# A selective-scan and expert block on one core: one more state scaled on ScalarE, one more product on GpSimd, the DMA queue and four copies re-ordered

## The chip, the core and the metric

The kernel runs on one core of one Trainium2 chip. The metric is the device time of one execution in microseconds (us); lower is better. The engines of the core run side by side and meet only at semaphores: TensorE (PE in the profile) multiplies matrices and transposes, VectorE (DVE) and ScalarE (ACT) work on tensors in the two on-chip memories SBUF and PSUM, GpSimd (POOL) on tensors in SBUF, and SyncE (SP) issues the DMAs. Each engine executes its own list of instructions in order, so an instruction that waits holds up everything behind it on its engine.

## The reference

The input x has 32 sequences of 512 tokens and 256 channels. It is normalised per token (xn), goes through a selective scan in both directions, and is gated by an expert feed-forward layer:

```python
dbc = einsum('bld,nd->bln', xn, x_proj_w); delta, B, C = split(dbc)      # 32 + 16 + 16
delta = softplus(einsum('blr,dr->bld', delta, dt_proj_w) + dt_proj_b)
h[t] = exp(delta[t] * A) * h[t-1] + delta[t] * B[t] * xn[t]              # 16 states, 256 channels
y    = sum over states (h * C) + D * xn       # forward, and again on the reversed sequence
out  = x + (y_forward + y_backward) * silu(ffn(xn))
```

`ffn` picks one of 8 experts per sequence (a router on the last token), and computes xn + 0.3 * ((gelu(xn W1 + b1) W2 + b2) Wo + bo). All of it is float32.

## The kernel before, in words

Channels lie on the 128 partitions in two halves (DT = 2), tokens along the free dimension, so one tensor for one state is 128x1024. There are 32 **sequences** (the code calls them rows), and in each of them 32 **states**, 16 forward and 16 backward, numbered 0 to 31. Each engine runs a loop over sequences and, inside, over 32 **steps** s; step s is mostly the work on state s. Into the steps the **front** of the next sequence is woven: its normalisation, its projections, its delta and its feed-forward layer. The tables at lines 37 to 49 say at which step each piece of the front is issued (a number of 32 or more is a step of the following sequence).

For one state the work is:

- **decay** (ACT, `make_decay`, L745): exp(delta * A), two instructions of 128x512, two states ahead of the scan. It goes to one of two PSUM buffers (`dps`, called decay in the profile), which is free once the scan two states earlier has ended; for a *turned* state it goes to SBUF (`decay_sb`).
- **bx** = delta * x * B, by one of two ways. For the states in POOL_B, GpSimd multiplies `dx` by a row of B that a DMA has spread over the partitions (`times_b`, L473). For the states in TURNED, ScalarE scales `dxT` (the transposed dx) by B in four instructions of 128x256 (`scale_dx`, L584, at the step that SCALED_AT gives) and TensorE transposes the result into the PSUM buffer (`turn_bx`, L1054, three steps ahead).
- **scan** (DVE, L849): h = decay * h + bx over the 1024 columns.
- **product with C**: for the states in ON_DVE, TensorE spreads C over the partitions of one PSUM bank (`broadcast_c`, L1062) and DVE multiplies (`times_c`, L827), after the scan of the next state. For the states in POOL_C, GpSimd multiplies with a row of C brought by a DMA (L461), four steps later in its own order.
- **sum** (PE, `add_state`, L1079): eight 128x128 matmuls add the product to y in PSUM.

The front pieces of one sequence share one PSUM bank, `fps` (front in the profile): TensorE fills it, ScalarE or VectorE copies it out, and only then does TensorE fill it again. The pieces that matter here, in their order: the expansion of delta for channel half q of the direction (`expand_delta`, L997 and L998), copied out by `absolute` (L592 writes |.| to ex, L596 writes the relu to delta); the feed-forward input (`ffn_in`, L1007), copied out by `hidden` (L619); and the transposes of dx (`turn_dx`, L983), copied out by `copy_dxT` (L574). On ScalarE, `drain` issues these copies at the start of a step, ahead of the decay and of `scale_dx`; `front` comes after them and holds the exp, ln and squares of softplus (L600, L605, L609, L613) and the gelu. On TensorE the front comes last in a step.

Ahead of the loops lies a prologue (from L698 on ScalarE): the router, the product W2 Wo for all eight experts (`turn_w2`, `times_wo`, `copy_w2o`), and the front of sequence 0.

SP issues all DMAs in one order: it walks over the states of POOL_B, loads B five products ahead and C three products ahead, each behind a wait for the product that frees the buffer, and at two places it adds the loads of the expert and the move of the projections (`move_bc`, which brings high and low into dbc).

## Time and profile before

| | |
|---|---|
| time, median of 3 | 3342.31 us (3339.49 to 3346.29) |
| the profiled execution | 3348.41 us, of which the trace spans 3346.6 us |
| DVE busy | 3116.1 us, 93% |
| POOL busy | 3010.0 us, 90% |
| ACT busy | 2908.7 us, 87% |
| PE busy (modelled ends) | 2561.6 us, 77% |
| mean granted TensorE clock | 0.916 of full speed |

DVE, POOL and ACT each have under 15% of the span in which they do nothing. Busy time that high on three engines means that the share alone does not tell what a change is worth: what tells it is which engine's wait ends last at the place that is changed. Mean times of one instruction are read from the rows below; on ACT, DVE and POOL an instruction starts some 0.1 us before the one ahead of it has ended, so the distance of two starts is the right cost of one.

### The profile page before, as it was taken

To read this page: it belongs to the slowest core of one execution; us is meant where nothing else is said; L and a number is where in the kernel's file an instruction comes from. 1 tells how busy PE (TensorE), PEld (TensorE's weight loads), DVE (VectorE), ACT (ScalarE), POOL (GpSimd) and SP (SyncE) were. 2 spreads that over 40 slices of the span, in tenths; PEclk is the share of its full clock that TensorE was granted. 3 is DMA by queue.
4 is the path that set the end of the run, shared out by engine and by line. 5 is a ranking of instruction groups with operands and counts; after the bars stand their busy time and mean duration, and the time that the engine had idled before them with its cause. 6 is when DMAs were issued, how large, how long until landed. Compare 5 with 4: busy or idle time off the path is not lost. (4 is left out here: it accounts for less than half of the span.)

```text
span 3346.6 us, 47865 instructions
## 1 busy us (share of the span) xinstructions
PE 2561.6 (77%) x15542; PEld 2049.9 (61%) x15542; DVE 3116.1 (93%) x2059; ACT 2908.7 (87%) x5370; POOL 3010.0 (90%) x1422
## 2 busy tenths in 40 slices
PE   7777777777777777777777777777777777777776
PEld 5666656666566665566666566666566665666665
DVE  2899999999999999999999999999999999999998
ACT  4888889989888888898888899898898888898985
POOL 2899999999998998999999999999999889999997
PEclk9898999899899988999889999988999889999888
DMA  5443344442344433434433444423434334344332
GB/s 155 137 125 104 100 138 121 128 124 88 119 131 125 125 109 95 132 121 128 125 103 101 136 122 125 126 91 115 130 128 125 106 93 136 119 130 124 96 104 69
DMA packets 273358, 394.09 MB, mean 118 GB/s; under 512 B 45003, under 2 KB 119508, under 8 KB 273108
## 3 DMA queue, kind: packets, MB, share of 16 engines
q1 hardware_dynamic: 273108, 391.03, 38.1%
q8 instruction: 124, 2.03, 0.2%
q14 instruction: 126, 1.03, 0.1%
HBM read 348.98 MB, written 25.18 MB: 112 GB/s over the span
## 5 line engine op out<-in xcount | busy, mean ns | idle before, releaser
L473 POOL TENSOR_TENSOR bx<-dx,b_sb 128x1024 f32<-128x1024 f32 x640 | 1511.8, 2380 | 99.5 <-DVE hs L849 97.7
L849 DVE TENSOR_TENSOR_SCAN hs<-decay,bx 128x1024 f32<-128x1024 f32 x640 | 1458.0, 2280 | 25.5 <-ACT decay L745 8.5
L1079 PE MATMUL y<-ident,hc 128*128 128x128 f32 x8192 | 1145.4, 291 | 25.7 <-DVE hc L827 25.5
L1079 PEld LDWEIGHTS y<-ident,hc 128*128 128x128 f32 x8192 | 1029.9, 152 | 141.2 <-DVE hc L827 80.1
L461 POOL TENSOR_TENSOR hc<-hs,c_sb 128x1024 f32<-128x1024 f32 x416 | 981.0, 2369 | 13.2 <-DVE hs L849 12.9
L849 DVE TENSOR_TENSOR_SCAN hs<-decay_sb,decay 128x1024 f32<-128x1024 f32 x384 | 865.1, 2274 | 77.1 <-issue 38.0
L745 ACT ACTIVATE decay<-delta,rate 128x512 f32<-128x512 f32 (+1 forms) x1280 | 827.3, 683 | 62.1 <-DVE hs L849 61.7
L827 DVE TENSOR_TENSOR hc<-hs,c 128x1024 f32<-128x1024 f32 x608 | 728.7, 1199 | 40.7 <-PE c L1062 36.8
L584 ACT ACTIVATE dxb<-dxT,btok 128x256 f32<-128x256 f32 x1536 | 651.2, 497 | 0.5 <-PE decay L1054 0.5
L1054 PE MATMUL decay<-ident,dxb 128*128 128x128 f32 x3072 | 435.5, 288 | 252.8 <-DVE hs L849 246.4
L1054 PEld LDWEIGHTS decay<-ident,dxb 128*128 128x128 f32 x3072 | 359.7, 147 | 367.5 <-issue 272.7
L1062 PE MATMUL c<-dbc,selector 128*128 128x512 f32 x608 | 327.0, 538 | 324.8 <-DVE hc L827 324.7
L745 ACT ACTIVATE decay_sb<-delta,rate 128x512 f32<-128x512 f32 (+1 forms) x768 | 506.2, 715 | 0.0
L1062 PEld LDWEIGHTS c<-dbc,selector 128*128 128x128 f32 x608 | 125.1, 206 | 407.8 <-DVE hc L827 389.7
L1023 PE MATMUL front<-w2o_sb,hT 128*128 128x256 f32 x1024 | 287.0, 430 | 77.9 <-issue 77.9
L1023 PEld LDWEIGHTS front<-w2o_sb,hT 128*128 128x128 f32 x1024 | 214.7, 221 | 114.2 <-issue 84.4
L1007 PE MATMUL front<-xnT,w_sb 128*128 128x512 f32 x512 | 249.9, 611 | 44.0 <-ACT delta L596 42.8
L448 POOL TENSOR_TENSOR lg<-lg,ex 128x1024 f32<-128x1024 f32 x64 | 151.1, 2362 | 86.9 <-ACT lg L613 86.9
L592 ACT ACTIVATE ex<-front,dtb 128x512 f32<-128x512 f32 x128 | 87.3, 682 | 100.0 <-PE front L998 99.6
L574 ACT ACTIVATE dxT<-front 128x512 f32<-128x512 f32 x128 | 75.8, 592 | 103.3 <-PE front L983 103.1
L619 ACT ACTIVATE hT<-front,b_sb 128x512 f32<-128x512 f32 x128 | 87.7, 685 | 87.3 <-PE front L1007 87.3
L1007 PEld LDWEIGHTS front<-xnT,w_sb 128*128 128x128 f32 x512 | 88.3, 192 | 121.6 <-issue 63.1
(127 smaller groups left out, 2294.4 us busy)
## 6 DMA issues: line engine op xcount, KB each, us to landing
b_sb<-b_scratch SPq DMA_DIRECT2D x640, 256.0 KB, 3.4
c_sb<-b_scratch SPq DMA_DIRECT2D x416, 256.0 KB, 3.6
xin<-in_L_attn_x_dram SPq DMA_DIRECT2D x32, 512.0 KB, 7.7
w_sb<-in_L_ffn_W_dram SPq DMA_DIRECT2D x32, 512.0 KB, 4.3
w2o_sb<-w2o_scratch SPq DMA_DIRECT2D x32, 512.0 KB
xres<-in_L_attn_x_dram SPq DMA_DIRECT2D x32, 512.0 KB, 5.4
out_dram<-og SPq DMA_DIRECT2D x32, 512.0 KB, 4.4
dbc<-high SPq DMA_DIRECT2D x64, 128.0 KB, 5.6
```

The costliest lines, as they stand in the source:

```text
L448: nc.gpsimd.tensor_tensor(lg[:, :, :], lg[:, :, :], ex[:, g, :, :], ALU.mult).then_inc(s_log1p, 1)
L461: nc.gpsimd.tensor_tensor(hc[:, s % RING, :, :], hs[:, s % HSLOTS, :, :], c_sb[:, i % CRING, :].unsqueeze(1).broadcast_to([P, DT, T]), ALU ...
L473: nc.gpsimd.tensor_tensor(bx[:, i % RING, :, :], dx[:, g, :, :], b_sb[:, i % BRING, :].unsqueeze(1).broadcast_to([P, DT, T]), ALU.mult).th ...
L584: A(dxb[:, (row * NT + i) % XSLOTS, c, :], dxT[:, g, c, :], ACT.Copy, scale=btok[:, par, c, g, n:n + 1]).then_inc(s_dxb, 1)
L745: A(to[:, k, cols], delta[:, g * (1 + par), k, cols], ACT.Exp, scale=rate[:, g, k, n:n + 1]).then_inc(s_decay, 1)
L827: V.tensor_tensor(hc[:, s % RING, :, :], hs[:, s % HSLOTS, :, :], cps[:, :].unsqueeze(1).broadcast_to([P, DT, T]), ALU.mult).then_inc(s_hc, 1)
L849: V.tensor_tensor_scan(hs[:, s % HSLOTS, :, :].rearrange("p k t -> p (k t)")[:, u], factor.rearrange("p k t -> p (k t)")[:, u], data.rearr ...
L1007: ins = M(fps[:, :], w1_sb[:, k, j * P:(j + 1) * P], xnT[:, par, k, :], start=(k == 0), stop=(k == DT - 1))
L1023: M(to, hT[:, j, c * P:(c + 1) * P], w2o_sb[:, j, :], start=(j == 0), stop=False)
L1054: ins = nc.tensor.transpose(dps[s % DSLOTS][:, k, c * P:(c + 1) * P], dxb[:, (row * NT + i) % XSLOTS, c, k * P:(k + 1) * P], ident[:, :])
L1062: M(cps[:, :], selector[:, N + n:N + n + 1].broadcast_to([P, P]), dbc[:, par, g, :], start=True, stop=True).then_inc(s_cps, 1)
L1079: ins = M(yps[:, c, k * P:(k + 1) * P], hc[:, s % RING, k, c * P:(c + 1) * P], ident[:, :], start=False, stop=(s == ADDED[-1]), is_transpo ...
```

## The change

State 20 joins TURNED (12 states become 13, scaled at step 15), so its bx moves from GpSimd to ScalarE and TensorE. State 17 joins POOL_C (13 become 14), so its product with C moves from DVE to GpSimd. Four copies out of the shared bank move: the two of the forward delta (ABS 16 and 17) from the start of their step to behind the decay and the scaling, HIDDEN's last from step 24 to 25, and the first two of DX_COPY from 30 and 31 to 31 and 32. SP's loop now walks over all 32 steps in GpSimd's order, and `move_bc` comes at step 14. In the prologue the gelu of sequence 0 goes behind the first two decays, the router's exp ahead of the first softplus, and the loads of the dt weights ahead of those of W2 and Wo. Lines behind the edits shift by 1 to 3.

```diff
-    DX_TURN, DX_COPY = (28, 29, 44, 45), (30, 31, 46, 47)
-    FFN_IN, HIDDEN, GELU = (16, 16, 18, 18, 20, 20, 22, 22), (18, 20, 22, 24), 31
+    DX_TURN, DX_COPY = (28, 29, 44, 45), (31, 32, 46, 47)
+    FFN_IN, HIDDEN, GELU = (16, 16, 18, 18, 20, 20, 22, 22), (18, 20, 22, 25), 31
...
-    TURNED, SCALED_AT, TURN_LEAD = (..., 15, 22, 24, 28, 30), (..., 10, 17, 19, 23, 25), 3
+    TURNED, SCALED_AT, TURN_LEAD = (..., 15, 20, 22, 24, 28, 30), (..., 10, 15, 17, 19, 23, 25), 3
-    POOL_C, C_LAG, ADD_LAG = (2, 4, 5, 7, 9, 10, 11, 12, 16, 18, 20, 26, 27), 4, 2
+    POOL_C, C_LAG, ADD_LAG = (2, 4, 5, 7, 9, 10, 11, 12, 16, 17, 18, 20, 26, 27), 4, 2
...
-            sp.dma_start(w2_in[0][:, :, :], w2_v[0]).then_inc(s_w2[0], 16)
-            sp.dma_start(wo_sb[:, :, :], wo.rearrange("(k p) n -> p k n", p=P)).then_inc(s_wo, 16)
             sp.wait_ge(s_dtz, 1)
...
+            sp.dma_start(w2_in[0][:, :, :], w2_v[0]).then_inc(s_w2[0], 16)
+            sp.dma_start(wo_sb[:, :, :], wo.rearrange("(k p) n -> p k n", p=P)).then_inc(s_wo, 16)
...
-                for i in range(NBX):
-                    j = i + BRING - 1
...
-                    for s in POOL_C:
-                        ahead = POOL_C.index(s) + C_AHEAD
-                        if on_bx(s) == i and ahead < NPC:
-                            load_c(row, par, ahead)
+                for s in range(STEPS):
+                    if s in POOL_B:
+                        j = on_bx(s) + BRING - 1
...
+                    if s - C_LAG in POOL_C:
+                        i = on_pool(s - C_LAG) + C_AHEAD
+                        if i < NPC:
+                            load_c(row, par, i)
...
-                    if POOL_B[i] == 16 and not last:
+                    if s == 14 and not last:
...
             def drain(row, par, s):
-                if s in DX_COPY:
+                if s in DX_COPY and (row or s in DX_COPY[DT:]):
                     copy_dxT(row, DX_COPY.index(s))
-                if s in ABS:
+                if s in ABS[DT:]:
                     absolute(row, par, ABS.index(s))
...
             def front(row, par, s):
...
+                if s in ABS[:DT]:
+                    absolute(row, par, ABS.index(s))
                 if s in EXP:
...
             absolute(0, 0, 1)
+            act.wait_ge(s_rv, 6)
+            A(lexp[:, :], router_ps[0:NB, 384:384 + NE], ACT.Exp, bias=lneg[:, :], accum_out=lsum[:, :]).then_inc(s_ra, 1)
             exp_abs(0, 0)
...
-            gelu(0)
-            act.preload_act_table_set(exp_ln)
             def make_decay(row, par, s):
...
             make_decay(0, 0, 1)
+            gelu(0)
+            act.preload_act_table_set(exp_ln)
```

How this changes the order on two engines, at steps 16 to 20 of a sequence. On ScalarE before, from the first copy of the forward delta (ex and delta are its two halves) to the decay of state 20 (decay0 and decay1 are the two PSUM buffers, dxb the scaled dx of state 22, hT the first piece of the feed-forward input):

```order
L592 ACTIVATE ex<-front,dtb 128x512
L596 ACTIVATE delta<-front,dtb 128x512
L745 ACTIVATE decay0<-delta,rate 128x511
L745 ACTIVATE decay0<-delta,rate 128x512
L592 ACTIVATE ex<-front,dtb 128x512
L596 ACTIVATE delta<-front,dtb 128x512
L745 ACTIVATE decay1<-delta,rate 128x511
L745 ACTIVATE decay1<-delta,rate 128x512
L584 ACTIVATE dxb<-dxT,btok 128x256 x4
L619 ACTIVATE hT<-front,b1_sb 128x512
L745 ACTIVATE decay0<-delta,rate 128x511
L745 ACTIVATE decay0<-delta,rate 128x512
```

The two pairs L592 and L596 stand ahead of the decays of states 18 and 19; between the second pair and hT there are a decay and a scaling. Now, on the same engine, from the decay of state 18 on:

```order
L746 ACTIVATE decay0<-delta,rate 128x511
L746 ACTIVATE decay0<-delta,rate 128x512
L593 ACTIVATE ex<-front,dtb 128x512
L597 ACTIVATE delta<-front,dtb 128x512
L746 ACTIVATE decay1<-delta,rate 128x511
L746 ACTIVATE decay1<-delta,rate 128x512
L585 ACTIVATE dxb<-dxT,btok 128x256 x4
L593 ACTIVATE ex<-front,dtb 128x512
L597 ACTIVATE delta<-front,dtb 128x512
L620 ACTIVATE hT<-front,b1_sb 128x512
L743 ACTIVATE decay_sb<-eps 128x1
L746 ACTIVATE decay_sb<-delta,rate 128x511
```

The second pair now stands directly ahead of hT, behind the decay of state 19 and the scaling of state 22, and the decay of state 20 goes to SBUF and has a small edge instruction (L743) of its own. On VectorE before, from the scan of state 16 to that of state 20 (the five L849 rows), with the products of states 15 and 17 between them:

```order
L849 SCALAR_TENSOR_TENSOR hs<-decay0,bx 128x1024
L827 TENSOR_TENSOR hc<-hs,c 128x1024
L849 SCALAR_TENSOR_TENSOR hs<-decay1,bx 128x1024
L849 SCALAR_TENSOR_TENSOR hs<-decay0,bx 128x1024
L827 TENSOR_TENSOR hc<-hs,c 128x1024
L849 SCALAR_TENSOR_TENSOR hs<-decay1,bx 128x1024
L849 SCALAR_TENSOR_TENSOR hs<-decay0,bx 128x1024
```

The fifth row is the product of state 17. Now the same engine from state 16 on:

```order
L852 SCALAR_TENSOR_TENSOR hs<-decay0,bx 128x1024
L830 TENSOR_TENSOR hc<-hs,c 128x1024
L852 SCALAR_TENSOR_TENSOR hs<-decay1,bx 128x1024
L852 SCALAR_TENSOR_TENSOR hs<-decay0,bx 128x1024
L852 SCALAR_TENSOR_TENSOR hs<-decay1,bx 128x1024
L852 SCALAR_TENSOR_TENSOR hs<-decay_sb,decay0 128x1024
```

The product is gone, and the scans of states 17 to 20 stand in a row; that of state 20 takes its decay from SBUF and its bx from the PSUM buffer.

## Rows read from the trace of the kernel before

**Rows 1.** The page's part 1: busy time, share of the span, instructions.
```profile
PE 2561.6 (77%) x15542; PEld 2049.9 (61%) x15542; DVE 3116.1 (93%) x2059; ACT 2908.7 (87%) x5370; POOL 3010.0 (90%) x1422
```

**Rows 2.** Waits by engine and releaser: us in total, times, longest us.
```profile
ACT hT L619 <- PE front L1007: 87.3, 37, 3.8
...
DVE hc L827 <- PE c L1062: 36.8, 33, 1.9
...
DVE zz L802 <- PE front L1025: 19.1, 33, 3.3
```

**Rows 3.** The page's part 5: busy us, mean ns; idle before, releaser.
```profile
L473 POOL TENSOR_TENSOR bx<-dx,b_sb 128x1024 f32<-128x1024 f32 x640 | 1511.8, 2380 | 99.5 <-DVE hs L849 97.7
L849 DVE TENSOR_TENSOR_SCAN hs<-decay,bx 128x1024 f32<-128x1024 f32 x640 | 1458.0, 2280 | 25.5 <-ACT decay L745 8.5
...
L849 DVE TENSOR_TENSOR_SCAN hs<-decay_sb,decay 128x1024 f32<-128x1024 f32 x384 | 865.1, 2274 | 77.1 <-issue 38.0
```

**Rows 4.** Durations at their extremes, by line: ns min/median/max, first and last start.
```profile
L820 DVE TENSOR_TENSOR og<-y,gate x32: 1198/1198/1226, 198.2 to 3339.5; 128x1024 f32<-128x1024 f32 x32
...
L849 DVE TENSOR_TENSOR_SCAN hs<-decay,bx x640: 2258/2282/2292, 84.3 to 3333.1; 128x1024 f32<-128x1024 f32 x160
```

**Rows 5.** Order of time, VectorE, 448 to 464 us: start, us, instruction, idle.
```profile
448.30 4.46 DVE L849 TENSOR_TENSOR_SCAN hs<-decay,bx 128x1024 f32<-128x1024 f32 x2
452.68 1.20 DVE L827 TENSOR_TENSOR hc<-hs,c 128x1024 f32<-128x1024 f32 x1
453.80 4.67 DVE L849 TENSOR_TENSOR_SCAN hs<-decay,bx 128x1024 f32<-128x1024 f32 x2
...
463.02 2.29 DVE L849 TENSOR_TENSOR_SCAN hs<-decay_sb,decay 128x1024 f32<-128x1024 f32 x1 [1.25 <-ACT decay_sb L745]
```

**Rows 6.** Order of time, ScalarE, the same stretch.
```profile
447.88 0.69 ACT L592 ACTIVATE ex<-front,dtb 128x512 f32<-128x512 f32 x1 [2.38 <-PE front L998]
...
450.26 0.68 ACT L592 ACTIVATE ex<-front,dtb 128x512 f32<-128x512 f32 x1
450.83 0.69 ACT L596 ACTIVATE delta<-front,dtb 128x512 f32<-128x512 f32 x1
451.40 1.31 ACT L745 ACTIVATE decay<-delta,rate 128x511 f32<-128x511 f32 x2
452.62 1.70 ACT L584 ACTIVATE dxb<-dxT,btok 128x256 f32<-128x256 f32 x4
454.22 0.68 ACT L619 ACTIVATE hT<-front,b_sb 128x512 f32<-128x512 f32 x1
...
461.39 0.21 ACT L742 ACTIVATE decay_sb<-eps 128x1 f32<-128x1 f32 x1
461.49 1.34 ACT L745 ACTIVATE decay_sb<-delta,rate 128x511 f32<-128x511 f32 x2
```

**Rows 7.** Order of time, TensorE, the same stretch.
```profile
451.57 1.98 PE L1007 MATMUL front<-xnT,w_sb 128*128 128x512 f32 x4 [1.34 <-ACT delta L596]
```

**Rows 8.** Order of time, all engines, the prologue.
```profile
10.76 0.66 PE L1106 MATMUL c<-ident,decay_sb 128*128 128x128 f32 x2 [10.76 <-DMA decay_sb<-_L_attn_dt_proj_b_w_dram]
...
45.48 0.15 DVE L900 RECIPROCAL lrec<-lsum 32x1 f32<-32x1 f32 x1 [5.68 <-ACT lexp L704]
...
78.08 1.29 DVE L858 COPY hc<-y 128x512 f32<-128x512 f32 x2 [7.68 <-PE y L1089]
...
84.30 2.29 DVE L849 TENSOR_TENSOR_SCAN hs<-decay,bx 128x1024 f32<-128x1024 f32 x1 [4.93 <-ACT decay L745]
```

**Rows 9.** The same matmuls at the half clock, and core 0's mean clock.
```profile
1060.58 3.45 PE L1007 MATMUL front<-xnT,w_sb 128*128 128x512 f32 x4 [1.41 <-ACT delta L596]
...
core 0: 3346.6 us, clock 0.916
```

**Rows 10.** Order of time, all engines, around a sequence's last state.
```profile
1102.21 0.60 ACT L574 ACTIVATE dxT<-front 128x512 f32<-128x512 f32 x1 [3.09 <-PE front L983]
...
1104.92 1.22 DVE L827 TENSOR_TENSOR hc<-hs,c 128x1024 f32<-128x1024 f32 x1 [1.11 <-PE c L1062]
```

More of the change, by code:

```diff
@@ L396, in body @@
                 first, second_last = isinstance(row, int) and row == 0, isinstance(row, int) and row == NB - 2
-                for i in range(NBX):
-                    j = i + BRING - 1
-                    if j < NBX:
-                        load_b(row, par, j)
-                    elif not last:
-                        load_b(row + 1, 1 - par, j - NBX)
-                    for s in POOL_C:
-                        ahead = POOL_C.index(s) + C_AHEAD
-                        if on_bx(s) == i and ahead < NPC:
-                            load_c(row, par, ahead)
-                        elif on_bx(s) == i and not last:
-                            load_c(row + 1, 1 - par, ahead - NPC)
-                    if POOL_B[i] == 10:
+                for s in range(STEPS):
+                    if s in POOL_B:
+                        j = on_bx(s) + BRING - 1
+                        if j < NBX:
+                            load_b(row, par, j)
+                        elif not last:
+                            load_b(row + 1, 1 - par, j - NBX)
+                    if s - C_LAG in POOL_C:
+                        i = on_pool(s - C_LAG) + C_AHEAD
+                        if i < NPC:
+                            load_c(row, par, i)
+                        elif not last:
+                            load_c(row + 1, 1 - par, i - NPC)
+                    if s == 10:
                         if not first:
@@ L425, in _ @@
         def _(pool):
+            nc.gpsimd.memset(dtw_raw[:, :, :, :], 0.0).then_inc(s_dtz, 1)
             nc.gpsimd.memset(ident[:, :], 0.0).then_inc(s_ident0, 1)
```

5 lines of the change are left out of this document (1 added, 4 removed).

## The prediction

> **What bounds the kernel now.** I read the busy shares first [rows 1]: VectorE 93%, GpSimd 90%, ScalarE 87%. The reader is to see that VectorE leads and that no engine has much room. Next came the waits [rows 2]: ScalarE waits 87.3 us for TensorE's feed-forward input, VectorE 36.8 us for the C that TensorE spreads and 19.1 us for the gate input. The costliest groups [rows 3] add that GpSimd's products with B wait 97.7 us for VectorE's scans, and that VectorE's scans have 25.5 and 77.1 us of idle ahead of them. So VectorE leads and the others mostly follow it. The 32 gate products `og` start between 198.2 and 3339.5 us [rows 4], so a sequence costs (3339.5 - 198.2) / 31 = 101.3 us.
>
> Then I read one sequence in order of time, where the change is, at 448 to 464 us [rows 5 to 7], on three engines. On VectorE, 448.30 x2 are the scans of states 17 and 18; 452.68 is the product of state 17, the one that the change takes away; 453.80 x2 are the scans of 19 and 20; behind those follow the product of 19 and state 21, and at 463.02 state 22, after 1.25 us of idle put down to ScalarE's decay. So at this place ScalarE's list, not VectorE, sets when state 22 starts. On ScalarE [rows 6] no instruction after 447.88 shows idle time ahead of it: pair L592/L596, decay 18, pair, decay 19, scaling of 22, hT, decay 20 and so on up to the decay of 22 at 461.49. The place is a local bound by ScalarE inside a kernel that VectorE bounds elsewhere.
>
> **The change part by part.** Distances of starts are the costs [rows 5, 6]: a product on VectorE 453.80 - 452.68 = 1.12 us; on ScalarE a pair of copies 451.40 - 450.26 = 1.14, a decay 452.62 - 451.40 = 1.22, a scaling 454.22 - 452.62 = 1.60, an edge instruction 461.49 - 461.39 = 0.10.
>
> *State 17's product leaves VectorE, state 20's bx leaves GpSimd, state 17's product joins GpSimd.* GpSimd is even. VectorE has 1.12 us less per sequence, all of it between the scans of 18 and 19. ScalarE gets four scalings, 1.60 us, at step 15, ahead of the decay of 18; that lies in the 2.38 us in which it waited for the first pair [rows 6], so it costs nothing by itself.
>
> *The copies of the forward delta move behind the decays.* This is the term that decides. I go through the same sequence with the new order. The decay of 18 now comes before the first pair, in the old idle time. The decay of 19 goes to the PSUM buffer that the scan of 17 reads, so it starts when that scan ends: 448.30 + 2.28 = 450.58. Then the scaling of 22 at 451.80, the second pair at 453.40, its relu half at 453.97 (0.57 later, as from 450.26 to 450.83). Before, that half started at 450.83. TensorE's first feed-forward group waits for this half: it started 451.57 - 450.83 = 0.74 after it and took 1.98 us [rows 7]. Before, that lay beside the decay of 19 and the scaling of 22. Now nothing stands between the pair and hT: hT is the next instruction of the list and waits for those matmuls, to 453.97 + 0.74 + 1.98 + 0.04 = 456.73. It stood at 454.22 [rows 6]: 2.51 us late. Behind it, in order, are the decay of 20, exp, the decay of 21, the scaling of 24, ln, the second hT and the decay of 22, which is what state 22 waits for. The decay of 20 also gets an edge instruction, 0.10. State 22 then starts at 463.02 + 2.51 + 0.10 = 465.63, 2.6 us later. On VectorE the three scans 18, 19 and 20 stand in a row: with 2.2 us each from 450.5 (448.30 + 4.46 - 2.26) the scan of 19 is over at 454.9. State 20's started at 453.80 + 4.67 - 2.28 = 456.19 and now starts at 456.19 + 2.61 = 458.8, so VectorE waits 3.9 us there, and the 1.12 us that the product gave up are inside this wait. 31 sequences have such a stretch (the last one has no next front): 31 x 2.61 = +81.
>
> *What that wait swallows.* Scans fed from bx have 25.5 us of idle ahead of them [rows 3], of which 4.93 belong to the first scan [rows 8]. The other 20.6 are waits of states 18, 20 and 26, which come from late pieces of the same chain; the new order puts the decay of 18 first and HIDDEN's last copy behind the decay of 26. I take all of it off: -21. The bounds are 0 and 21.
>
> *The half clock.* The mean granted clock is 0.916 [rows 9], so (1 - 0.916) x 2 = 17% of the time is at 1.2 GHz. There the group of matmuls that is now exposed takes 3.45 us and not 1.98 [rows 7, 9]: 31 x 0.17 x 1.47 = +8, between 0 and twice that.
>
> *The last sequence* saves its product: -1.
>
> *The two DX_COPY.* The first stood at step 30 and waited 3.09 us for its transposes [rows 10]; at step 31 it comes behind a decay (1.3 with its edge) and a square (1.1) and lands at about the same time. Zero, because ScalarE's idle time hides it; if that cover were gone, the product of state 31, which has 1.11 us of idle ahead of it [rows 10], would come later by what the copy is late, at most some 0.5 us per sequence, +16. The reordering of HIDDEN's last copy is in the 21 above.
>
> *SP's order.* It issues the same DMAs. `move_bc` now waits for less, but what it feeds, the first pair, is no longer what is late. What holds GpSimd's products with B up is a scan in 97.7 of 99.5 us [rows 3], not a DMA, and the new order asks for each buffer when GpSimd has freed it. Zero; queued behind a wait in it are the B and C rows of the steps ahead, five and three products early.
>
> *The prologue.* The first scan waits 4.93 us for its decay behind the gelu and its two table loads, and VectorE is free after the copy that ends at 79.37 [rows 8]. It will start up to 4.6 us earlier; but the gelu now lies ahead of the decay of state 2, and gives most of it back. The router's exp comes four softplus instructions earlier, where VectorE waited 5.68 us, and TensorE's first transposes waited to 10.76 us for the dt weights, which now load ahead of W2. Bounds: 0, and 4.93 + 5.68 + half of 10.76 = -16. I take -6, nearer to the lower end since each of the three meets the next wait.
>
> **Sum**: 81 - 21 + 8 - 1 - 6 = +61 us. Against the profiled execution, 3348.4 us (span 3346.6 and 1.8 around it), that is 3409. The median of the runs is 6.1 below the profiled one, so the median should be 3342.3 + 61 = 3403 us, 1.8% slower.
>
> **The rivals.**
>
> *VectorE's relief counts in full* (the other side). The one mechanism: hT does not wait, because the wait at state 20 stays below what VectorE has gained. The place is the stretch of rows 5, the price is 32 x 1.12 = -36 us plus -6 in the prologue, and it decides from the point where hT starts less than 1.1 us later than it did, that is, if the pair would stand at 452.0 and not at 453.4. For it: the busy shares, where VectorE leads. Against it: ScalarE's list stands in a fixed order, and its costs are all from rows. 3342 - 42 = 3300 us.
>
> *The late start is made up later*. The stretch is late by 2.6 us, but VectorE waits elsewhere as well: 36.8 us for the spread C and 19.1 for the gate input [rows 2]. If these fell to nothing and the prologue gave its full 16 us: 61 - 56 - 10 = -5, about 3337 to 3345. Against it: most of them come from chains that start at a scan of VectorE and so move with it.
>
> *The moved product stops VectorE.* Both engines read SBUF, and a GpSimd product of 2.37 us more beside the scans could hold a scan up for its length. In the trace 640 scans take 2258 to 2292 ns [rows 4] beside a GpSimd that is busy 90% of the time [rows 1], so no such hold is seen. If each of the 32 moved products did hold one up: 32 x (2.37 - 1.12) = +40, about 3382 us with the stretch as it was. The Trainium skill (Perfetto Trace Analysis, section "Optimizing Scalar/DVE Operations") warns that VectorE and GpSimd share a read port, so that moving work between those two might not help; by that rule the move of the product is worth nothing or less, and the trace does not bear it out for these operand kinds.
>
> *The change does not do what it says*: the order of the two kernels shows that it does, so this has no chance of its own.
>
> **How the numbers follow.** The forecast, a new wait ahead of state 20, has 77%. Its own range goes from +26 (the waits for C fall to their floor of about 0.65 us, the 0.48 us matmul and its hand-over, and those for the gate input vanish: 61 - 17 - 19) to +90 (no cover, half clock twice as frequent): 3365 to 3432 us, which I take to hold nine in ten of it. VectorE's relief in full 13%, made up later 5%, the moved product or a starved queue 5%. The range is to leave out no more than two in ten: 3330 to 3430. About 0.2% (7 us) is what a measurement of this kernel can tell from no change. Faster comes from the relief, 13%; the same from the case that is made up, 5%; slower from the rest, 82%.
>
> **What the profile after would show.** Right: idle time ahead of the scans that read decay_sb grows from 77.1 us [rows 3] by about 31 x 3.9 = 120 us, put down to ScalarE's decay_sb or to issue; in a sequence the scan of 20 starts some 8.2 us after the end of the scan of 17, and that of 22 some 15.0 after it, against 5.6 and 12.4; ScalarE waits about 2 us for TensorE ahead of the first hT of each sequence, and no longer ahead of the first pair; VectorE's busy time falls by 36 us. GpSimd's idle time grows by 2 us a sequence. Right for the other steps: the first scan starts near 79 us or before. Wrong: if no wait over 1 us stands ahead of state 20's scan, the term of 81 is wrong; if it stands there and the sequence is still not longer than 101.3 us, what swallows it is what I left out.

## The result and the profile after

The changed kernel takes 3455.81 us (median of 4 runs, 3451.8 to 3457.05) against 3344.3 us of the kernel before (4 runs, 3339.49 to 3356.89): 1.0325 times as long, 95% interval 1.0295 to 1.0356. That is 111 us more, where 61 were forecast. The sign was right; the time lies 26 us above the range's upper end. The times and ratios in this document leave out a second, longer time that one kernel showed: two of the five runs of e1_copies_ahead, the traced one among them, took 3365 us and not 3312, for a reason that no run here tells.

The page's part 1 of the changed kernel, as in [rows 1], and its row of the granted clock in tenths, one digit for a fortieth of the span:

```profile
PE 2596.1 (75%) x15766; PEld 2061.1 (60%) x15766; DVE 3076.1 (89%) x2027; ACT 2983.1 (86%) x5498; POOL 3010.8 (87%) x1422
...
PEclk9989899899999899999989999988999899989998
```

VectorE lost 40 us of work (3116.1 to 3076.1) and its share fell from 93% to 89%: nothing on it got slower, it waits. Its waits come next, with those of the engines that it waits for: us in total, times, longest.

```profile
DVE hs L852 <- ACT decay_sb L746: 214.1, 64, 5.8
...
ACT hT L620 <- PE front L1010: 143.7, 64, 9.7
...
PE front L1010 <- ACT delta L597: 129.2, 31, 4.2
...
DVE hs L852 <- issue: 36.7, 63, 0.8
...
DVE hc L830 <- PE c L1065: 34.5, 28, 1.4
...
ACT ex L593 <- PE front L1001: 20.6, 34, 1.8
...
DVE zz L805 <- PE front L1028: 15.6, 27, 3.3
```

VectorE's waits for C and for the gate input are nearly what they were in [rows 2] (36.8 and 19.1). New is a chain of three: TensorE waits up to 4.2 us for the delta, ScalarE 143.7 us for TensorE's feed-forward input (87.3 before), and VectorE up to 5.8 us for ScalarE's decay. The costliest groups that answer to [rows 3], with busy us, mean ns, then idle time ahead of them:

```profile
L474 POOL TENSOR_TENSOR bx<-dx,b_sb 128x1024 f32<-128x1024 f32 x608 | 1435.7, 2377 | 89.3 <-DVE hs L852 89.1
L852 DVE TENSOR_TENSOR_SCAN hs<-decay,bx 128x1024 f32<-128x1024 f32 x608 | 1378.4, 2276 | 4.4 <-ACT decay L746 3.8
L462 POOL TENSOR_TENSOR hc<-hs,c_sb 128x1024 f32<-128x1024 f32 x448 | 1052.8, 2363 | 142.1 <-DVE hs L852 141.7
L852 DVE TENSOR_TENSOR_SCAN hs<-decay_sb,decay 128x1024 f32<-128x1024 f32 x416 | 937.6, 2273 | 250.5 <-ACT decay_sb L746 214.1
...
L1010 PE MATMUL front<-xnT,w_sb 128*128 128x512 f32 x512 | 300.2, 717 | 136.3 <-ACT delta L597 129.2
```

The idle time ahead of the scans that read decay_sb went from 77.1 to 250.5 us, ahead of those that read bx from 25.5 to 4.4. A scan takes what it took (2276 and 2273 ns against 2280 and 2274). State 20 counts among the readers of decay_sb only since the change; its waits are 178.8 of the 250.5 us. The last row is the group whose price the prediction had too low: TensorE's feed-forward matmuls take 717 ns each in the mean, and they took 611 before.

One sequence in order of time shows where that comes from. VectorE, as in [rows 5]: three scans in a row (states 17, 18, 19), 5.82 us of waiting ahead of state 20, and 1.10 ahead of state 22.

```profile
458.17 6.64 DVE L852 TENSOR_TENSOR_SCAN hs<-decay,bx 128x1024 f32<-128x1024 f32 x3
470.63 2.29 DVE L852 TENSOR_TENSOR_SCAN hs<-decay_sb,decay 128x1024 f32<-128x1024 f32 x1 [5.82 <-ACT decay_sb L746]
...
477.33 2.29 DVE L852 TENSOR_TENSOR_SCAN hs<-decay_sb,decay 128x1024 f32<-128x1024 f32 x1 [1.10 <-ACT decay_sb L746]
```

ScalarE in the same stretch, as in [rows 6]. The second pair (463.32, 463.89) is directly followed by hT, which waits 3.87 us.

```profile
460.49 1.30 ACT L746 ACTIVATE decay<-delta,rate 128x511 f32<-128x511 f32 x2 [0.83 <-DVE hs L852]
461.73 1.69 ACT L585 ACTIVATE dxb<-dxT,btok 128x256 f32<-128x256 f32 x4
463.32 0.67 ACT L593 ACTIVATE ex<-front,dtb 128x512 f32<-128x512 f32 x1
463.89 0.67 ACT L597 ACTIVATE delta<-front,dtb 128x512 f32<-128x512 f32 x1
468.44 0.69 ACT L620 ACTIVATE hT<-front,b_sb 128x512 f32<-128x512 f32 x1 [3.87 <-PE front L1010]
469.02 0.19 ACT L743 ACTIVATE decay_sb<-eps 128x1 f32<-128x1 f32 x1
469.12 1.32 ACT L746 ACTIVATE decay_sb<-delta,rate 128x511 f32<-128x511 f32 x2
```

TensorE in it, as in [rows 7]. After its last small matmul at 460.06 it has nothing to do for 4.17 us, and then the four matmuls that all others wait for take 3.78 us, not 1.98.

```profile
460.06 0.39 PE L1001 MATMUL front<-dbc,dtw_low 128*128 128x512 f32 x1
464.62 3.78 PE L1010 MATMUL front<-xnT,w_sb 128*128 128x512 f32 x4 [4.17 <-ACT delta L597]
468.19 1.76 PE L1057 MATMUL decay<-ident,dxb 128*128 128x128 f32 x8
```

The same place by stretches: us, then busy time of TensorE, its weight loads, VectorE, ScalarE and GpSimd, the granted clock, DMA share, GB/s.

```profile
460.00:463.00 3.00, 0.45 (x2) 0.01 (x1) 3.00 (x3) 2.51 (x6) 3.00 (x2) 0.97 0.36 119
463.00:466.00 3.00, 1.38 (x2) 0.84 (x3) 1.81 (x1) 1.56 (x4) 3.00 (x2) 0.50 0.31 108
466.00:469.00 3.00, 3.00 (x7) 1.37 (x6) 0.00 (x0) 0.56 (x1) 2.82 (x2) 0.50 0.20 68
469.00:472.00 3.00, 3.00 (x18) 2.40 (x17) 1.36 (x1) 3.00 (x7) 0.00 (x0) 0.89 0.26 87
```

The granted clock is 0.97, then 0.50 (1.2 GHz) in two stretches of three microseconds each, and in them lie all four matmuls that the kernel waits for. In the kernel before it is 1.00 throughout this place, where TensorE idled 1.34 us:

```profile
448.00:451.00 3.00, 1.78 (x11) 1.31 (x11) 3.00 (x3) 3.00 (x6) 3.00 (x3) 1.00 0.44 139
451.00:454.00 3.00, 2.05 (x5) 0.75 (x6) 3.00 (x3) 3.00 (x7) 3.00 (x2) 1.00 0.04 16
```

The group is slow in every sequence. Of the 31 such groups of matmuls, 26 take 3.78 us in the changed kernel and the other five 3.26 to 3.51; in the kernel before, 27 took 1.98 or 1.99 and only four were slow (3.23 to 3.48). Yet the mean clock of the whole span hardly moved (0.916 before, 0.912 now). From the first scan of the second sequence to the first scan of the last one, thirty sequences on, a sequence now takes (3352.568 - 193.755) / 30 = 105.29 us, against (3242.964 - 191.656) / 30 = 101.71 before.

### The profile page after: what moved, and what is told of

The parts are those of the page before. It is cut to its first block and busy times, and to the rows that moved or that the text cites. A ratio compares the mean times of both kernels' runs of the same rounds, so it can differ in the third digit from the quotient of the medians.

```text
span 3455.1 us, 48409 instructions
## 1 busy us (share of the span) xinstructions
PE 2596.1 (75%) x15766; PEld 2061.1 (60%) x15766; DVE 3076.1 (89%) x2027; ACT 2983.1 (86%) x5498; POOL 3010.8 (87%) x1422
## 5 line engine op out<-in xcount | busy, mean ns | idle before, releaser
L474 POOL TENSOR_TENSOR bx<-dx,b_sb 128x1024 f32<-128x1024 f32 x608 | 1435.7, 2377 | 89.3 <-DVE hs L852 89.1
L852 DVE TENSOR_TENSOR_SCAN hs<-decay,bx 128x1024 f32<-128x1024 f32 x608 | 1378.4, 2276 | 4.4 <-ACT decay L746 3.8
L462 POOL TENSOR_TENSOR hc<-hs,c_sb 128x1024 f32<-128x1024 f32 x448 | 1052.8, 2363 | 142.1 <-DVE hs L852 141.7
L852 DVE TENSOR_TENSOR_SCAN hs<-decay_sb,decay 128x1024 f32<-128x1024 f32 x416 | 937.6, 2273 | 250.5 <-ACT decay_sb L746 214.1
L746 ACT ACTIVATE decay<-delta,rate 128x511 f32<-128x511 f32 (+1 forms) x1216 | 786.4, 680 | 180.8 <-DVE hs L852 180.4
L830 DVE TENSOR_TENSOR hc<-hs,c 128x1024 f32<-128x1024 f32 x576 | 689.5, 1197 | 39.8 <-PE c L1065 34.5
L585 ACT ACTIVATE dxb<-dxT,btok 128x256 f32<-128x256 f32 x1664 | 704.6, 495 | 0.0
L746 ACT ACTIVATE decay_sb<-delta,rate 128x512 f32<-128x512 f32 (+1 forms) x832 | 547.6, 712 | 0.0
L1010 PE MATMUL front<-xnT,w_sb 128*128 128x512 f32 x512 | 300.2, 717 | 136.3 <-ACT delta L597 129.2
L620 ACT ACTIVATE hT<-front,b_sb 128x512 f32<-128x512 f32 x128 | 87.0, 680 | 143.7 <-PE front L1010 143.7
L445 POOL TENSOR_TENSOR dx<-delta,xnT 128x1024 f32<-128x1024 f32 x64 | 151.9, 2373 | 2.5
L454 POOL TENSOR_TENSOR delta<-lg,delta 128x1024 f32<-128x1024 f32 x64 | 151.6, 2369 | 0.1
```

The source lines that it names most:

```text
L445: nc.gpsimd.tensor_tensor(dx[:, g, :, :], delta[:, g * (1 + par), :, :], xnT[:, par, :, :], ALU.mult).then_inc(s_dx, 1)
L462: nc.gpsimd.tensor_tensor(hc[:, s % RING, :, :], hs[:, s % HSLOTS, :, :], c_sb[:, i % CRING, :].unsqueeze(1).broadcast_to([P, DT, T]), ALU ...
L474: nc.gpsimd.tensor_tensor(bx[:, i % RING, :, :], dx[:, g, :, :], b_sb[:, i % BRING, :].unsqueeze(1).broadcast_to([P, DT, T]), ALU.mult).th ...
L585: A(dxb[:, (row * NT + i) % XSLOTS, c, :], dxT[:, g, c, :], ACT.Copy, scale=btok[:, par, c, g, n:n + 1]).then_inc(s_dxb, 1)
L746: A(to[:, k, cols], delta[:, g * (1 + par), k, cols], ACT.Exp, scale=rate[:, g, k, n:n + 1]).then_inc(s_decay, 1)
L830: V.tensor_tensor(hc[:, s % RING, :, :], hs[:, s % HSLOTS, :, :], cps[:, :].unsqueeze(1).broadcast_to([P, DT, T]), ALU.mult).then_inc(s_hc, 1)
```

## The experiments

Twelve kernels ran. They ask which part of the change costs the time, why it costs twice what was forecast, and what the parts are worth without it. Ratios are to the kernel before on the same chip, with 95% intervals.

### Which part costs the time

**e2_copies_only**: the kernel before with this part alone.

```diff
             def drain(row, par, s):
-                if s in ABS:
+                if s in ABS[DT:]:
                     absolute(row, par, ABS.index(s))
             def front(row, par, s):
+                if s in ABS[:DT]:
+                    absolute(row, par, ABS.index(s))
                 if s in EXP:
```

> The kernel before with one part added: the two copies of the forward delta behind the decay and the scaling; nothing else. Theory: this alone brings the whole loss, 31 x (16.8 - 12.9) = +120 us, 3440 to 3470 us, with the clock low while the first feed-forward matmuls run; if the clock were high there, 31 x 2.0 = +62, 3404 us. Rival (the states): within 20 us of the kernel before.

Measured: 3466.51 us, 1.0355 [1.0335, 1.0374]. This part alone brings the whole loss, as expected (3440 to 3470 us). The ratio is some 10 us above that of the full change, but the two intervals overlap. The trace has a trap for readers. Its wait is labelled with GpSimd's bx:

```profile
471.00 2.29 DVE L851 TENSOR_TENSOR_SCAN hs<-decay,bx 128x1024 f32<-128x1024 f32 x1 [4.46 <-POOL bx L473]
```

```profile
468.06 2.36 POOL L473 TENSOR_TENSOR bx<-dx,b_sb 128x1024 f32<-128x1024 f32 x1
```

```profile
469.04 0.69 ACT L619 ACTIVATE hT<-front,b_sb 128x512 f32<-128x512 f32 x1 [3.87 <-PE front L1009]
469.62 1.29 ACT L747 ACTIVATE decay<-delta,rate 128x511 f32<-128x511 f32 x2
```

The bx was ready at 468.06 + 2.36 = 470.42, the decay of state 20 at 469.62 + 1.29 = 470.91, and the scan starts at 471.00. So the scan follows ScalarE's decay, behind the same late hT, though GpSimd was only 0.5 us ahead of it.

**e1_copies_ahead**: the changed kernel with this part alone undone, so all the others remain.

```diff
-                if s in ABS[DT:]:
+                if s in ABS:
                     absolute(row, par, ABS.index(s))
...
-                if s in ABS[:DT]:
-                    absolute(row, par, ABS.index(s))
                 if s in EXP:
```

> The changed kernel with one part undone: the two copies of the forward delta stand at the start of steps 16 and 17 again, ahead of the decay and the scaling. Theory (the place of the copies): the first hT no longer waits for the matmuls, the wait ahead of state 20's scan falls from 5.8 us to under 1, state 22 starts 12.9 us after the end of the scan of 17 and not 16.9, and the kernel takes 3315 to 3340 us. Rival (the states that moved, through the four added scalings and state 20's decay in SBUF): the time stays above 3430 us.

Measured: 3312.57 us, 0.9897 [0.9878, 0.9917], 2 us below the range that was expected. Nothing is read from its trace. With e2 it brackets the part: -143 us if it is undone, +120 if it is done alone. The remaining parts together are worth some -34.

**e4_states_only**: the kernel before with the tables of states, 13 scaled on ScalarE and 14 products on GpSimd.

```diff
-    TURNED, SCALED_AT, TURN_LEAD = (..., 15, 22, 24, 28, 30), (..., 10, 17, 19, 23, 25), 3
+    TURNED, SCALED_AT, TURN_LEAD = (..., 15, 20, 22, 24, 28, 30), (..., 10, 15, 17, 19, 23, 25), 3
-    POOL_C, C_LAG, ADD_LAG = (..., 16, 18, 20, 26, 27), 4, 2
+    POOL_C, C_LAG, ADD_LAG = (..., 16, 17, 18, 20, 26, 27), 4, 2
```

> The kernel before with the tables of states alone changed: 13 states scaled on ScalarE, 14 products with C on GpSimd; all copies, the queue and the prologue as before. Theory (the stretch from the first copy to the decay of state 22 is bound by ScalarE's list): the 1.12 us less on VectorE per sequence brings nothing, since state 22 waits for ScalarE, and the scalings ahead of the first copy cost 0 to 0.4 us per sequence: 3340 to 3355 us. Rival (VectorE bounds the stretch): 31 x 1.1 = 35 us less, 3308 us.

Measured: 3349.23 us (10 runs), 1.0007 [0.9994, 1.0019]. VectorE's busy time falls to 3082.5 us, 34 less, and the time does not move. The answer is in one row: the idle time ahead of the scans that read decay_sb, state 20 now among them, went from 77.1 [rows 3] to 122.1 us. The edit moves the product and adds ScalarE's scalings at once, so it prices the two together and neither alone. It also isn't free of the clock: ten of the 31 feed-forward groups are slow in this trace (3.42 to 3.64 us), against four before. With such a group state 20 waits 2.1 to 2.4 us, without it 1.3, so six more of them are some 6 us.

```profile
L849 DVE TENSOR_TENSOR_SCAN hs<-decay_sb,decay 128x1024 f32<-128x1024 f32 x416 | 937.7, 2273 | 122.1 <-ACT decay_sb L745 79.1
```

**e5_queue_only**: the kernel before with SP's DMAs asked for in GpSimd's step order.

```diff
-                for i in range(NBX):
-                    j = i + BRING - 1
...
-                    for s in POOL_C:
-                        ahead = POOL_C.index(s) + C_AHEAD
-                        if on_bx(s) == i and ahead < NPC:
-                            load_c(row, par, ahead)
...
+                for s in range(STEPS):
+                    if s in POOL_B:
+                        j = on_bx(s) + BRING - 1
...
+                    if s - C_LAG in POOL_C:
+                        i = on_pool(s - C_LAG) + C_AHEAD
...
-                    if POOL_B[i] == 16 and not last:
+                    if s == 14 and not last:
```

> The kernel before with SP's loop in GpSimd's step order and the move of the projections at step 14. Theory (no DMA was late for GpSimd; only the projections come earlier, which in some sequences held the first copy of delta up by about 1 us): 0 to 15 us less, 3330 to 3345 us. Rival (a B or C row now comes late): 10 us or more slower.

Measured: 3328.3 us, 0.9958 [0.9945, 0.9971]: 14 us (0.42%) faster, where the prediction had zero and the expectation 0 to 15. Of the two edits, the loop and the earlier `move_bc`, no run tells which one gains. The idle time ahead of the scans that read bx fell from 25.5 to 13.6 us:

```profile
L850 DVE TENSOR_TENSOR_SCAN hs<-decay,bx 128x1024 f32<-128x1024 f32 x640 | 1455.2, 2278 | 13.6 <-ACT decay L746 8.9
```

**e6_prologue_only**: the kernel before with row 0's gelu behind the decay of state 1, the router's exp earlier, and the dt weights loaded ahead of W2 (with GpSimd's clearing of their buffer at the head of its list).

```diff
-            gelu(0)
-            act.preload_act_table_set(exp_ln)
             def make_decay(row, par, s):
...
             make_decay(0, 0, 1)
+            gelu(0)
+            act.preload_act_table_set(exp_ln)
```

> The kernel before with the edits of the prologue alone: gelu behind the first decays, the router's exp earlier, the dt weights ahead of W2 and Wo. Theory (from the changed kernel's trace, where the first scan starts 4.0 us earlier and the first sequence takes 2.5 us more than the others gained): 1 to 5 us less. Forecast term: 6 us less, bounds 0 and 16.

Measured: 3342.09 us (12 runs), 0.9996 [0.9985, 1.0007]: nothing that can be told from noise; 1 to 5 us were expected. In its trace the first scan comes 2.9 us earlier than in [rows 8], at 81.42, and a later one waits 2.41 us behind the gelu; the first sequence takes 109.4 us and not 107.4:

```profile
81.42 2.29 DVE L849 TENSOR_TENSOR_SCAN hs<-decay,bx 128x1024 f32<-128x1024 f32 x1 [0.29 <-ACT decay L743]
...
92.31 2.29 DVE L849 TENSOR_TENSOR_SCAN hs<-decay,bx 128x1024 f32<-128x1024 f32 x1 [2.41 <-ACT decay L743]
```

**e7_late_copies_only**: the kernel before with the two copies of dx and the last copy of HIDDEN one step later, behind a decay.

```diff
-    DX_TURN, DX_COPY = (28, 29, 44, 45), (30, 31, 46, 47)
-    FFN_IN, HIDDEN, GELU = (16, 16, 18, 18, 20, 20, 22, 22), (18, 20, 22, 24), 31
+    DX_TURN, DX_COPY = (28, 29, 44, 45), (31, 32, 46, 47)
+    FFN_IN, HIDDEN, GELU = (16, 16, 18, 18, 20, 20, 22, 22), (18, 20, 22, 25), 31
...
-                if s in DX_COPY:
+                if s in DX_COPY and (row or s in DX_COPY[DT:]):
                     copy_dxT(row, DX_COPY.index(s))
```

> The kernel before with the first two DX_COPY at steps 31 and 32 and HIDDEN's last copy at step 25. Theory: the waits ahead of state 26 go (0.7 us in about a sixth of the sequences) and nothing else: 0 to 10 us less. Rival (the product of state 31 comes later because TensorE's second transpose waits for the later copy): 5 to 16 us more.

Measured: 3322.62 us, 0.9938 [0.9925, 0.9951]: 20 us faster, twice the upper end of what was expected. ScalarE's wait for TensorE ahead of the dx copies fell from 103.1 to 15.9 us, and the scans that read bx wait 8.8 us in place of 25.5.

```profile
ACT dxT L574 <- PE front L983: 15.9, 50, 0.7
```

```profile
L849 DVE TENSOR_TENSOR_SCAN hs<-decay,bx 128x1024 f32<-128x1024 f32 x640 | 1454.9, 2278 | 8.8 <-ACT decay L745 4.9
```

So the same kind of move (a copy put behind a decay) gains here and loses at states 18 and 19. In both places the copy stood ahead of a decay *while it waited* for TensorE, and the move puts that wait behind what VectorE needs. The difference lies in what comes next: behind the forward delta's second pair comes hT, which waits for what that pair sets off.

The waits ahead of states 18 and 20 went as well, a dozen states away. The traces show a way, which no run tests: the dx copies stand in ScalarE's list ahead of the small instructions that make rsq, which stand near the beginning of the front of the sequence after. GpSimd's wait for rsq fell from 106.2 to 56.0 us, so that front starts earlier, and the pair at state 18 with it.

```profile
POOL nwt L487 <- ACT rsq L540: 56.0, 32, 6.0
```

### Why it costs twice the forecast

**e3_pe_kept_busy**: the changed kernel, with ten spare matmuls on TensorE at step 16, which spread the C of state 19 over its buffer again and again. They add work and take none away.

```diff
+                    if s == 16 and not last:
+                        wait(pe, s_hc, row * ND + on_dve(19))
+                        for _ in range(10):
+                            M(cps[:, :], selector[:, N + 3:N + 4].broadcast_to([P, P]), dbc[:, par, 1, :], start=True, stop=True)
                     front(row, par, s + STEPS, last)
```

> The changed kernel with ten more matmuls on TensorE in each of 31 sequences, ahead of the first feed-forward matmuls: the spread of C for state 19, written ten more times into a bank that nobody reads at that time, so that TensorE works while it would wait for the relu. Theory (TensorE's idle time of 4.2 us lets the clock fall, and that is what the forecast left out): the granted clock at the first feed-forward matmuls is high, they take 2.0 us and not 3.8, state 20's wait falls from 5.8 to 4.0 us, and the kernel takes 31 x 1.8 = 56 us less, 3400 us. Rival (the clock there is low for another reason, or the matmuls are slow for another): the time stays at 3456 us or rises.

Measured: 3420.71 us, 1.0219 [1.0202, 1.0237]; 35 us less than the changed kernel, by adding work. The expectation (3400) was missed by 20 us, and the trace shows that the edit did only half of what it was for: 1.86 us of idle time are left, and the clock still fell within most of the groups.

```profile
458.00 2.48 PE L1203 MATMUL c<-dbc,selector 128*128 128x512 f32 x10
462.34 2.47 PE L1010 MATMUL front<-xnT,w_sb 128*128 128x512 f32 x4 [1.86 <-ACT delta L597]
```

Only 6 of the 31 groups take 1.98 or 1.99 us; the others take 2.41 to 3.40.

**e8_pe_kept_busy_longer**: the same with sixteen.

```diff
-                        for _ in range(10):
+                        for _ in range(16):
```

> As the kernel with ten spare matmuls per sequence on TensorE, but with sixteen. The ten took 2.5 us and left 1.9 us of idle time, and the clock still fell in most sequences (wait of state 20: 4.4 to 5.5 us; only some had 4.0). Theory (idle time of TensorE ahead of the feed-forward matmuls brings the clock down): sixteen fill 4.0 of 4.2 us, the wait falls to about 4.0 us in nearly all sequences, 3395 to 3405 us. Rival (the clock falls whatever stands there): no faster than the 3421 us of ten, and above 3425 us if the longer fill delays the feed-forward matmuls.

Measured: 3403.33 us (3400.2 to 3403.59), 1.0171 [1.014, 1.0202]. TensorE now idles 0.51 us ahead of the feed-forward group, the granted clock is 1.00 there, and all 31 groups take 1.98 or 1.99 us.

```profile
453.83 3.83 PE L1203 MATMUL c<-dbc,selector 128*128 128x512 f32 x16
458.17 1.98 PE L1010 MATMUL front<-xnT,w_sb 128*128 128x512 f32 x4 [0.51 <-ACT delta L597]
```

```profile
451.72 6.64 DVE L852 TENSOR_TENSOR_SCAN hs<-decay,bx 128x1024 f32<-128x1024 f32 x3
462.39 2.29 DVE L852 TENSOR_TENSOR_SCAN hs<-decay_sb,decay 128x1024 f32<-128x1024 f32 x1 [4.04 <-ACT decay_sb L746]
```

State 20 waits 4.04 us, where the prediction worked out 3.9. The kernel is the changed one in every other part, so the slow clock accounts for 3455.8 - 3403.3 = 52.5 us (by the two ratios 1.54%, 51 us). Three amounts of spare work agree with this: with none, ten and sixteen matmuls the group takes 3.73, 2.72 and 1.98 us in the mean, and the kernel 3456, 3421 and 3403. Without the slow clock the loss is 1.71%, 57 us, and the forecast without its term for the clock is 61 - 8 = 53.

**e11_hidden_behind_decay**: the changed kernel with the first hT behind the decay of state 20, so that the wait for TensorE stands behind what VectorE needs.

```diff
-                if s in HIDDEN:
+                if s in HIDDEN[1:]:
                     hidden(row, HIDDEN.index(s))
...
+                if s == HIDDEN[0]:
+                    hidden(row, 0)
                 if s in EXP:
```

> The changed kernel, with the first hT of a sequence behind the decay of state 20 on ScalarE in place of ahead of it; the copies of delta stay where the change put them. Theory (ScalarE's in-order list carries hT's wait to the decay): state 20 starts 5.5 us after the scan of 17 and not 10.2; hT is still at 8.0, and state 22 then starts at 16.9 less the 1.3 us decay that has gone ahead, 15.6: 31 x 1.3 = 41 us less than the changed kernel, 3415 us. Rival (state 20 waits for its transposes on TensorE, behind the slow matmuls): state 20 stays near 10 us, and the time at 3450 us.

Measured: 3412.77 us (four runs, 3402.93 to 3421.18), 1.0192 [1.0155, 1.023]. The time is as expected, the reason given for it is only half right: state 22 comes earlier as said, but state 20 still waits 4.4 to 5.2 us, now for TensorE.

```profile
466.45 2.29 DVE L854 TENSOR_TENSOR_SCAN hs<-decay_sb,decay 128x1024 f32<-128x1024 f32 x1 [5.02 <-PE decay L1059]
```

```profile
461.22 3.78 PE L1012 MATMUL front<-xnT,w_sb 128*128 128x512 f32 x4 [4.17 <-ACT delta L597]
464.80 1.61 PE L1059 MATMUL decay<-ident,dxb 128*128 128x128 f32 x8
```

```profile
461.17 1.32 ACT L748 ACTIVATE decay_sb<-delta,rate 128x511 f32<-128x511 f32 x2
```

The decay is there at 462.5, four microseconds before the scan. But the scan also takes its bx from PSUM, and the transposes that write it stand in TensorE's list behind the slow matmuls. The late pair delays state 20 through two lists, ScalarE's and TensorE's.

### What the parts give without the wait

**e9_first_hidden_late**: e1 (copies ahead again), the first hT behind the decay of state 20 as in e11, and the scaling of state 24 at step 21.

```diff
-    TURNED, SCALED_AT, TURN_LEAD = (..., 28, 30), (..., 15, 17, 19, 23, 25), 3
+    TURNED, SCALED_AT, TURN_LEAD = (..., 28, 30), (..., 15, 17, 21, 23, 25), 3
...
-                if s in ABS[DT:]:
+                if s in ABS:
                     absolute(row, par, ABS.index(s))
-                if s in HIDDEN:
+                if s in HIDDEN[1:]:
                     hidden(row, HIDDEN.index(s))
...
-                if s in ABS[:DT]:
-                    absolute(row, par, ABS.index(s))
+                if s == HIDDEN[0]:
+                    hidden(row, 0)
```

> A version meant to be fast: the copies of delta back ahead of the decays (3312.6 us so far), the first hT behind the decay of state 20, and the scaling of state 24 at step 21 in place of 19. Theory (what is left in the stretch is ScalarE's list, 1.3 us ahead of state 20 and 1.1 ahead of 22): both waits fall below 0.5 us, 31 x 1.5 = 46 us less, 3265 to 3290 us. Rival (VectorE already has no room, or the scaling at 21 makes TensorE's transposes late): 3310 us or more.

Measured: 3260.04 us (3259.16 to 3265.0), 0.9745 [0.9716, 0.9774], 89 us faster than the kernel before and 5 below the range that was expected. State 20 waits 0.75 us and state 22 not at all, all 31 feed-forward groups take 1.98 or 1.99 us, and the granted clock is 0.945 in the mean.

```profile
448.47 2.29 DVE L852 TENSOR_TENSOR_SCAN hs<-decay_sb,decay 128x1024 f32<-128x1024 f32 x1 [0.75 <-ACT decay_sb L746]
```

**e10_spread**: e9 with the scaling of state 22 and the forward softplus pieces one step later.

```diff
-    EXP, LN, SQUARE, RATIO = (18, 27), (19, 28), (20, 29), (21, 30)
+    EXP, LN, SQUARE, RATIO = (19, 27), (20, 28), (21, 29), (22, 30)
-    TURNED, SCALED_AT, TURN_LEAD = (..., 28, 30), (..., 15, 17, 21, 23, 25), 3
+    TURNED, SCALED_AT, TURN_LEAD = (..., 28, 30), (..., 15, 18, 21, 23, 25), 3
```

> The same version with more of ScalarE's work out of the stretch: also the scaling of state 22 at step 18 in place of 17, and exp, ln and both squares of the forward delta one step later each. Theory: the waits ahead of 20 and 22 vanish, 31 x 2.4 = 74 us less than 3312.6, down to 3240 us, if GpSimd, which waits 1.5 to 3 us per sequence for the last square already, absorbs one that is 2 us later. Rival (GpSimd or a later decay takes the place of the wait): 3290 us or more.

Measured: 3263.01 us, 0.9753 [0.9724, 0.9782]: no gain over e9, where 3240 us were expected. The wait at state 20 is gone, and two others, ahead of scans that wait for GpSimd, took its place, 31 times each:

```profile
DVE hs L852 <- POOL bx L474: 24.3, 31, 0.8
...
DVE hs L852 <- POOL hc L462: 10.6, 31, 0.4
```

**e12_states_back**: e9 with the tables of states of the kernel before (12 scaled, 13 products).

```diff
-    TURNED, SCALED_AT, TURN_LEAD = (..., 15, 20, 22, 24, 28, 30), (..., 10, 15, 17, 21, 23, 25), 3
+    TURNED, SCALED_AT, TURN_LEAD = (..., 15, 22, 24, 28, 30), (..., 10, 17, 21, 23, 25), 3
-    POOL_C, C_LAG, ADD_LAG = (..., 16, 17, 18, 20, 26, 27), 4, 2
+    POOL_C, C_LAG, ADD_LAG = (..., 16, 18, 20, 26, 27), 4, 2
```

> The fast version (copies ahead, first hT behind the decay of state 20, scaling of 24 at step 21; 3260 us) with the states as in the kernel before: 12 scaled on ScalarE, 13 products on GpSimd. Theory (once ScalarE does not bind the stretch, VectorE's product counts in full): 31 x 1.1 = 35 us more than 3260, less what VectorE still waits for ahead of state 20 (0.76 us per sequence, 23 us): 3272 to 3295 us. Rival (moving the states is worth nothing anywhere): 3255 to 3265 us.

Measured: 3261.91 us, 0.9761 [0.9748, 0.9773], the same as e9 within the intervals. The expected loss did not come. VectorE has 29 us more work again (3107.6 against 3078.4) and some 25 us less idle time ahead of the scans that read decay_sb, first in e9, then in e12:

```profile
L852 DVE TENSOR_TENSOR_SCAN hs<-decay_sb,decay 128x1024 f32<-128x1024 f32 x416 | 937.6, 2273 | 61.8 <-issue 35.8
```

```profile
L852 DVE TENSOR_TENSOR_SCAN hs<-decay_sb,decay 128x1024 f32<-128x1024 f32 x384 | 864.0, 2270 | 37.3 <-issue 35.8
```

Moving the two states buys idle time on VectorE and nothing else, here as in e4: in e9 ScalarE, which then has the scalings of state 20 too, makes state 20 wait 0.75 us, and in e12 that wait is gone.

## Why the prediction was right in sign and wrong in size

**The deciding term, +81: right.** The chain came out as worked. From the end of the scan of state 17 (458.17 + 2.28 = 460.45) the relu half of the second pair starts 3.44 us later (forecast 453.97 - 450.58 = 3.39) and the matmuls 0.73 after that (0.74). At full clock, in e8, state 20's scan starts 462.39 - 454.00 = 8.4 us after that point (forecast 8.2) and state 22's 15.1 (forecast 15.0), and the whole loss is 57 us, where the forecast without its clock term has 53. That match of the totals is partly luck, since the small terms below are off in both directions; that e8 takes 3403 us, the very number of the forecast, is luck too, since the forecast has 8 us for the clock in it. The place, the releaser, the missing wait ahead of the first pair (none shown at 458.42, 2.38 before) and VectorE's lost busy time (40, forecast 36) are as predicted. e2 shows that this part alone is enough.

**The half clock, +8: the step that failed.** The prediction took the mean clock of the span, said that 17% of the time is slow, and charged 17% of the groups with 1.47 us. That treats the slow clock as weather that falls on the kernel independently of the change. But the term before had just moved the pair 3.14 us later (450.83 to 453.97) and had left TensorE's earlier work where it was. TensorE's idle time ahead of the group had to grow from 1.34 us to 1.34 + 3.14 = 4.48, and it is 4.17. In the trace the clock falls to 0.50 in that gap, in 26 of 31 sequences at the full price: 3.78 - 1.98 = 1.80 us each, so hT starts 7.99 us after the end of scan 17, not 6.15, and state 20 waits 5.82, not 3.9. 31 x 1.80 = 56, or 54 with the five groups that are slow in part; e8 measures 52.5. The bound given for the term (twice 8) was wrong for the same reason. Had it been "every sequence" at the price of [rows 9], 31 x 1.47 = 46, the sum would have been 3441. The Trainium skill (TensorE: Matmul & The Clock Gate, section "Why this matters for your kernels") advises against idle gaps between bursts of matmuls because they bring the clock back to half. The trace after and e8 agree; e3, where 25 of 31 groups take 2.41 us or more behind 1.86 us of idle time, and e4, where ten take 3.42 us or more behind 1.6, show it behind shorter gaps as well.

**What the wait swallows, -21: about right.** Before, the scan of state 22 started 12.93 us after the end of scan 17 in the mean and 12.43 where nothing else was late, so 0.50 x 31 = 15 us of small waits went inside the new one. Elsewhere in the sequence the new kernel gains 0.33 us, 10 in all.

**SP's order, 0, and the late copies, 0 beyond the 21: too cautious.** Alone they gain 14 and 20 us (e5, e7), and e1, which holds both, gains 34. Little of that shows in the full change: both remove the waits ahead of states 18 and 20, and the copies behind the decays remove these too (in e2's trace none is left ahead of state 18 or 26), so this gain and the term before are in part the same microseconds. Of the reason for the zero of SP's order (97.7 of 99.5 us of GpSimd's waits are for a scan) the row is right, but it spoke of the products with B only.

**The prologue, -6: nothing.** e6 measures 0.9996, with 1 inside its interval. The first scan did start early (80.32 in the changed kernel, 81.42 in e6), and the gelu took it back at a later state, as the prediction's own sentence had it. The lower end, 0, was the answer.

**The states, 0 for the scalings: not refuted.** e4 and e12 show that the moved product and the added scalings together are worth nothing, with the long wait and without it. What each is worth alone no run tells.

**The sum by the two traces.** The first scan starts 4.0 us earlier, the first sequence is 6.1 longer (113.4 us against 107.4), thirty periods bring 30 x 3.58 = 107.5, and the last sequence -1.1: 108.5, which is the difference of the spans (3455.1 - 3346.6).

**The rivals.** VectorE's relief in full is refuted by the wait at state 20. The late start was not made up later: the waits for C and for the gate input stayed at 34.5 and 15.6 us. The moved product stopped no scan: in the changed kernel the scans that read bx and have GpSimd working beside them for over nine tenths of their time (535) take 2275 ns in the mean, and those with it beside them for less than a tenth (22) take 2282. So the shared port that the Trainium skill warns of (Perfetto Trace Analysis, section "Optimizing Scalar/DVE Operations") does not show for these operands, though its conclusion, that such a move might not help, holds here for another reason. A slip in the sum of the range changes nothing: 61 - 17 - 19 is 25, so its own lower end is 3367, not 3365.

**What stays open.** Whether e7 removes the waits of states 18 and 20 in the way that its trace suggests. Which part of e5 gains. And what makes the clock fall behind some short gaps and not behind others: spare matmuls both shorten the gap and add work ahead of it, and e3 and e8 don't tell the two apart.

## What to carry to other kernels

In a list that is worked off in order, a copy must not move to directly ahead of the instruction that waits for what the copy sets off: the work between them was the cover of the round trip. When a step is moved later, work out the idle time that this leaves on TensorE ahead of the next matmuls, and charge those matmuls at the slow clock in every repetition where it grows as here (1.34 to 4.17 us), not at the mean clock of the span. And busy time taken off the leading engine is worth nothing until the trace shows that this engine, not another one's list, ends the wait at that place.

## What the runs showed of the hardware

- Spare matmuls can make a kernel faster: sixteen more per sequence, 3.83 us of TensorE's time, took 52.5 us off the changed kernel (e8); it stays 1.7% slower than the kernel before. With them the feed-forward group ran at 1.00 in place of 0.50, in 1.98 us and not 3.78.
- With 4.17 us of idle time ahead of the same group of matmuls, TensorE's granted clock fell in the gap or within the group in all 31 sequences. In e3, with 1.86 us of idle behind ten busy matmuls, 25 of 31 groups took 2.41 to 3.40 us. But the length of the gap alone does not tell: with 0.46 to 0.51 us (e8) and 1.56 to 1.58 (e9, e10) none was slow, with 1.33 to 1.41 (before) four, with 1.56 to 1.64 (e4) ten.
- The mean clock hides this: 0.916 and 0.912 stand for four slow groups of 31 and for 31 of 31. And runs of e10 at a mean clock of 0.913 and of 0.943 took 3262.4 and 3263.6 us. What counts is whether the slow stretch falls on matmuls that are waited for.
- Scans of 128x1024 on VectorE took no longer with a busy GpSimd beside them (2275 ns) than without (2282).
